# A transformer block's first stage: other engines for its casts and its normalisation, and the next stage's first loads issued inside it

## The chip, the core and the metric

The kernel runs on one core of a Trainium2 chip, as one program. The metric is the device time of one execution in microseconds (us); lower is better. Times here come from several executions of the kernel before and from one more that the hardware profiler recorded.

## What is computed

The input x has 2 sequences of 2048 tokens with 128 features. The first part of the reference is causal attention with 16 heads of 8 features on the layer-normalised x; a mixture-of-experts layer, a scan over time with four-lane attention, and a second mixture-of-experts layer follow, each with a residual connection. The change touches what feeds the attention and the attention's start:

```
xn = layernorm(x)                       # 4096 x 128
q = xn @ Wq.T + bq ;  k = xn @ Wk.T + bk ;  v = xn @ Wv.T + bv
scores = q k^T / sqrt(8), causal
out = softmax(scores) @ v ;  y = out @ Wo.T + bo
```

The product of queries and keys is taken in bf16, with each of q and k split into three bf16 parts (high, middle, low) whose products are summed, so that the result has the precision of float32.

## The kernel before, in words

`hybrid_layer` calls its stages one after the other: `project`, `attend`, `project_out`, then the others. Each stage is a block with one instruction stream for each engine, written by hand; semaphores order them, and an all-engine barrier ends each stage. `stage_semaphores` also clears the semaphores of its stage at its end.

**`project`** works on 8 chunks of 512 tokens (4 tiles of 128). SyncE issues the loads of x (8 chunks, counted on one semaphore for each half), of the weights and of the biases. VectorE takes the statistics of each half (L200, L55 to L61) and the reciprocal of the deviation (L205), whose root is ScalarE's (L251). For each chunk:

- GpSimd normalises x in two instructions (L173 subtracts the mean, L176 multiplies);
- TensorE transposes the four tiles (L290); ScalarE copies the result out of PSUM (L258);
- TensorE projects to q and to k (L295, one matmul of 512 columns each, which runs as two passes) and to v (L299, four matmuls of 128 columns);
- ScalarE writes the high bf16 part of q and of k with bias (L263), and again in float32 (`full`, L265);
- VectorE subtracts the high part from `full` (`rest`, L217), casts it to the middle part (L220), and computes q's low part (L223); GpSimd computes k's (L181);
- VectorE adds the bias to v (L226);
- SyncE stores the three parts of q and of k to DRAM (L133).

TensorE's order for a chunk is: transposes, both projections, values. The loops run dynamically over two times four chunks. The scan's weight is normalised on the side (`norm`, `S_pair`).

**`attend`** goes over 32 heads. For one head, the parts of q and k lie as 48 rows in a stack in SBUF (`Qs`, `Ks`; three stacks in rotation), loaded from DRAM by 12 DMAs (L452). TensorE scores each tile once to find the row maxima (L625, VectorE's L547), and the next time for the exponentials (L615, ScalarE's L593). The maxima pass of head s+1 runs beside the exponentials of head s; for head 0 it runs alone. After 12 of its 40 maxima VectorE reduces and casts them (L523, L526, L528). At the stage's start GpSimd fills buffers (L496, L500), adds the output bias to x in one instruction over 128x4096 elements (L504), and then stages v; TensorE and VectorE wait for all the fills.

The lines that say the order of VectorE's work on a chunk, before:

```
rest[a] = full[a] - parts[a, 0]      # a = 0, 1
parts[a, 1] = rest[a]
parts[0, 2] = rest[0] - parts[0, 1]  # a = 0 only
V = psV + bv_rows
```

## Time and profile before

| | |
|---|---|
| runs | 1838.46, 1840.71, 1843.89 us (median 1840.71) |
| profiled execution, its own time | 1842.67 us |
| its span, first to last instruction | 1840.9 us |
| mean granted TensorE clock | 0.917 of 2.4 GHz |
| busy share: TensorE matmul, VectorE, ScalarE, GpSimd | 84%, 75%, 52%, 34% |
| `project` | 0 to about 69 us |
| `attend` from | 70.31 us |

Times in the profile are microseconds from the span's start. PE is TensorE's matmuls and PEld its weight loads, DVE is VectorE, ACT is ScalarE, POOL is GpSimd, SPq is SyncE's queue. A matmul's end is modelled. PEclk is the granted clock: 1.00 is 2.4 GHz, 0.50 is 1.2 GHz; the record begins at 1.00 and shows no lower value before 56 us, although the first matmuls have the durations of the lower level. Names such as L217 are lines of the kernel.

### The profile page before, as it was taken

The page shows a single profiled execution, that of the slowest core. Times are in us where ns is not written, and L with a number is a line of the kernel's source. Part 1 is how long each engine was busy: PE and PEld are TensorE (multiplying, and loading weights), DVE is VectorE, ACT ScalarE, POOL GpSimd, SP SyncE. Part 2 cuts the span into 40 slices and gives each one's busy share as a digit, 9 for nine tenths or more (in the row PEclk, how much of TensorE's full clock was granted, in tenths as well). Part 3 has the DMA queues.
Part 4 walks back from the last instruction along what each step waited for, and adds up shares of the span by engine and source line. Part 5 has one row for each costly group of instructions (what it writes and reads, how often), then busy time and mean ns, then how long its engine had stood idle before and what let it go on. Part 6 is the DMA issues. An engine that isn't in the chain of part 4 may idle for free. (4 is left out here: it accounts for less than half of the span.)

```text
span 1840.9 us, 42069 instructions
## 1 busy us (share of the span) xinstructions
PE 1552.6 (84%) x13714; PEld 1007.8 (55%) x13714; DVE 1375.7 (75%) x2511; ACT 959.9 (52%) x2309; POOL 630.9 (34%) x430
## 2 busy tenths in 40 slices
PE   4599999999999999999950965999999999975267
PEld 2233333333333333333450955899999999965166
DVE  6799998998998998999261324788888888875222
ACT  4268877887887887888610322344444444431111
POOL 4500000000000000000036332888888888833534
PEclk9689999999999999999955987999999999986588
DMA  3300000000000000000084313011121222104740
GB/s 107 105 19 17 14 20 20 20 20 13 19 20 20 20 20 12 20 20 11 1 272 163 90 35 84 24 46 46 48 54 47 46 46 46 46 12 158 240 123 26
DMA packets 82116, 99.88 MB, mean 54 GB/s; under 512 B 12109, under 2 KB 65482, under 8 KB 81681
## 3 DMA queue, kind: packets, MB, share of 16 engines
q1 hardware_dynamic: 76816, 85.36, 16.0%
q0 software_dynamic: 5120, 12.26, 1.8%
q8 instruction: 97, 1.59, 0.4%
q14 instruction: 83, 0.67, 0.1%
HBM read 43.01 MB, written 31.85 MB: 41 GB/s over the span
## 5 line engine op out<-in xcount | busy, mean ns | idle before, releaser
L547 DVE TENSOR_REDUCE chunk_max<-ps_max 128x1 f32<-128x512 f32 (+3 forms) x1280 | 695.2, 604 | 64.1 <-PE ps_max L642 53.6
L593 ACT ACTIVATE probs<-ps_s 128x512 f32<-128x512 f32 (+3 forms) x1280 | 607.0, 533 | 175.0 <-PE ps_s L634 146.8
L1447 POOL TENSOR_TENSOR lane_products<-L,q 128x1024 f32<-128x1024 f32 x176 | 411.7, 2374 | 119.9 <-POOLq L1254 48.2
L615 PE MATMUL ps_s<-Qs,Ks 50*128 50x512 bf16 (+3 forms) x1280 | 377.2, 354 | 31.7 <-issue 12.1
L625 PE MATMUL ps_max<-Ks,Qs 48*128 48x512 bf16 (+3 forms) x1280 | 386.2, 361 | 12.8 <-POOL Vp L500 10.0
L688 PE MATMUL ps_o<-probs,Vp 128*32 128x512 f32 (+3 forms) x2560 | 344.4, 564 | 3.3 <-ACT probs L593 0.4
L615 PEld LDWEIGHTS ps_s<-Qs,Ks 50*128 50x128 bf16 x1280 | 113.8, 93 | 385.1 <-DVE chunk_max L547 327.6
L511 POOL COPY Vp<-V 128x128 f32 (+1 forms) x32 | 9.6, 300 | 741.2 <-PE ps_o L688 741.2
L1496 DVE TENSOR_TENSOR weighted<-exp_scores,psV_s 128x2048 f32<-128x2048 f32 x88 | 197.0, 2280 | 0.0
L1589 PE MATMUL psZT<-ident,weighted 128*128 128x128 f32 x1408 | 165.7, 273 | 1.8 <-DVE weighted L1496 1.8
L1589 PEld LDWEIGHTS psZT<-ident,weighted 128*128 128x128 f32 x1408 | 156.4, 140 | 2.0 <-DVE weighted L1496 2.0
L1575 PE MATMUL psS<-ident,lane_products 128*128 128x128 f32 x1056 | 128.1, 279 | 3.1 <-POOL lane_products L1447 3.1
L625 PEld LDWEIGHTS ps_max<-Ks,Qs 48*128 48x128 bf16 x1280 | 114.7, 94 | 24.1 <-DVE chunk_max L547 13.0
L1575 PEld LDWEIGHTS psS<-ident,lane_products 128*128 128x128 f32 x1056 | 124.2, 194 | 3.3 <-POOL lane_products L1447 3.3
L642 PE MATMUL ps_max<-ident_b,causal 64*128 64x64 bf16 x1024 | 115.6, 193 | 0.0
L634 PE MATMUL ps_s<-ident_b,causal 64*128 64x64 bf16 x1024 | 114.0, 192 | 0.0
L634 PEld LDWEIGHTS ps_s<-ident_b,causal 64*128 64x128 bf16 x1024 | 93.3, 97 | 23.7 <-issue 2.7
L1633 PE MATMUL psV_s<-S_pair,UT 128*128 128x128 f32 x704 | 97.4, 282 | 1.3 <-DVE weighted L1496 1.0
L642 PEld LDWEIGHTS ps_max<-ident_b,causal 64*128 64x128 bf16 x1024 | 94.5, 99 | 5.5 <-issue 2.0
L1633 PEld LDWEIGHTS psV_s<-S_pair,UT 128*128 128x128 f32 x704 | 85.9, 193 | 9.3 <-ACT UT L1527 7.2
L688 PEld LDWEIGHTS ps_o<-probs,Vp 128*32 128x32 f32 x2560 | 51.1, 109 | 72.2 <-issue 28.3
L1604 PE MATMUL psU<-ident,L 128*128 128x128 f32 x352 | 84.0, 279 | 5.8 <-PEq L1254 3.4
(220 smaller groups left out, 2160.4 us busy)
## 6 DMA issues: line engine op xcount, KB each, us to landing
m_w<-in_L_ffn_w_dram SPq DMA_DIRECT2D x32, 512.0 KB
dispatched<-m_blank SPq DMA_DIRECT2D x2, 4128.0 KB
m_blank<-dispatched SPq DMA_DIRECT2D x16, 516.0 KB
L<-q SPq DMA_DIRECT2D x16, 448.0 KB
Qs<-q_parts SPq DMA_DIRECT2D x192, 32.0 KB
Ks<-k_parts SPq DMA_DIRECT2D x192, 32.0 KB
L<-q SPq DMA_DIRECT2D x20, 192.0 KB
L<-q SPq DMA_DIRECT2D x28, 128.0 KB
```

Of the source, the lines that this page charges most:

```text
L547: nc.vector.tensor_reduce(out, scores[:, 0:w], axis=AX.X, op=ALU.max).then_inc(max_reduced, 1)
L593: nc.scalar.activation(dst, ps_s[(k + r) % R][:, q0:], ACT.Exp, scale=SCALE).then_inc(exp_done, 1)
L615: last = nc.tensor.matmul(ps_s[(k + r) % R][:, q0:], K[r][rows, kt * P:(kt + 1) * P], Q[r][rows, g * QW + q0:(g + 1) * QW], start=True, st ...
L625: last = nc.tensor.matmul(ps_max[(k + r) % R][:, 0:w], Q[r][rows, i * P:(i + 1) * P], K[r][rows, ck * QW:ck * QW + w], start=True, stop=no ...
L634: last = nc.tensor.matmul(ps_s[(k + r) % R][:, q0:q0 + HALF], c.causal[rows, 0, half, :], c.ident_b[rows, rows], start=False, stop=half == 1)
L642: last = nc.tensor.matmul(ps_max[(k + r) % R][:, k0:k0 + HALF], c.causal[rows, 1, half, :], c.ident_b[rows, rows], start=False, stop=half ...
L688: last = nc.tensor.matmul(ps_o[32 * q:32 * q + 32, q0:], Vp[r][:, kt, cols], src, start=first and not odd, stop=last_batch and odd)
L1447: return nc.gpsimd.tensor_tensor(out[:, l].rearrange("p (j m) d -> p j m d", m=LA), c.L[ch][:, :, l * LW:(l + 1) * LW].unsqueeze(2).broadc ...
L1496: nc.vector.tensor_tensor(weighted[v][:, rows], expd[:, :, rows].rearrange("p l r -> p r l").unsqueeze(3) .broadcast_to([P, ROWS // 2, LA, ...
L1575: nc.tensor.matmul(psS[:, 0:P], products[:, :, d], c.ident[:], start=d == PART, stop=False, is_transpose=True)
L1589: last = nc.tensor.matmul(psZT[:, j * P:(j + 1) * P], weighted[u][:, j * LA + m, :, :].rearrange("p l d -> p (l d)"), c.ident[:], start=m ...
L1633: last = nc.tensor.matmul(psV[:, j * D:(j + 1) * D], c.UT[u][:, j * P:(j + 1) * P], c.S[:, 0, :], start=True, stop=True)
```

## The change

In `project`:

- x is normalised by VectorE, one instruction for each tile of 128 tokens (`normalise`, in the new kernel L218), instead of by GpSimd. Chunks 0 and 1 are normalised ahead of the loop, chunk n+2 behind the values of chunk n.
- ScalarE no longer writes `full`; VectorE takes the rest directly from PSUM (scalar_tensor_tensor: PSUM plus bias, minus high part, L226). ScalarE casts the rest to the middle part.
- GpSimd computes the low part of both q and k.
- TensorE transposes chunk n+1 ahead of projecting chunk n.
- Loads of x are counted chunk by chunk; the second half's come behind the weights; the rows of the value bias come last. The second half's statistics stand behind the normalisation of the first two chunks. The table of ScalarE's functions is loaded once.
- The loops are unrolled, and buffers are waited for only once they have been used.
- SyncE issues the loads of heads 0, 1 and 2 at the stage's end, behind its stores.

In `attend` those loads go, the buffers' fills are in another order, VectorE waits for the first three of them only, and TensorE for none until head 0's exponentials. The stacks and their semaphores are now taken with the attention's tensors (`attention_tensors`), whose own scope ends after `project_out`.

```diff
+def load_head(sp, c, q_parts, k_parts, s, r, p):
+    rows, cols = bass.ds(s % H * HD, HD), bass.ds(s // H * T, T)
+    for stack, parts, order in ((c.Q[r], q_parts, (0, 0, 0, 1, 1, 2)), (c.K[r], k_parts, (0, 1, 2, 0, 1, 0))):
+        for row, a in enumerate(order):
+            sp.dma_start(stack[p * HALF + row * HD:p * HALF + (row + 1) * HD, :], parts[a, rows, cols])\
+              .then_inc(c.stacks_loaded[r], 16)
...
         @block.sync
...
+            load_x(0)
             for m, w in enumerate((Wq, Wk, Wv, Wo)):
                 sp.dma_start(W_nat[:, m, :], w).then_inc(w_loaded, 16)
...
+            load_x(1)
             sp.dma_start(bv_rows[:], bv.rearrange("(a d) -> a d", a=1).broadcast_to([P, D])).then_inc(b_loaded, 16)
...
+            for k in range(SLOTS):
+                sp.wait_ge(stored[k], 32)
+            for s in range(STACKS):
+                load_head(sp, c, q_parts, k_parts, s, s, s % 2)
+            for k in range(SLOTS):
+                sp.wait_ge(stored[k], 32 * (NCH // SLOTS))
...
         @block.gpsimd
...
             for ch in range(NCH):
-                if ch + 2 < NCH:
-                    normalise(ch + 2, ch % 2)
-                last_part(ch, ch % 4)
+                for a in range(2):
+                    part = parts[ch % SLOTS]
+                    pool.wait_ge(mid_done, 2 * ch + a + 1)
+                    nc.gpsimd.tensor_tensor(part[:, a, 2, :], rest[ch % 2][:, a, :], part[:, a, 1, :], ALU.subtract)\
+                      .then_inc(lo_done, 1)
...
         @block.vector
...
+            def normalise(ch):
+                dve.wait_ge(rstd_done, ch // CB + 1)
+                if ch >= 2:
+                    dve.wait_ge(xT_in_psum, ch - 1)
+                for i in range(TC):
+                    t = ch * TC + i
+                    last = nc.vector.tensor_scalar(xn[ch % 2][:, i, :], c.X[:, t, :], mean[:, t:t + 1],
+                                                   rstd[:, t:t + 1], ALU.subtract, ALU.mult)
+                last.then_inc(xn_ready, 1)
...
+                nc.vector.scalar_tensor_tensor(out=rest[ch % 2][:, a, :], in0=psQK[ch % 2][a][:],
+                                               scalar=bias_cols[:, a:a + 1], in1=parts[ch % SLOTS][:, a, 0, :],
+                                               op0=ALU.add, op1=ALU.subtract).then_inc(rest_done, 1)
...
+            for ch in range(NCH):
+                for a in range(2):
+                    rest_of(ch, a)
+                values(ch)
...
+                if ch + 2 < NCH:
+                    normalise(ch + 2)
...
         @block.scalar
...
+            act.wait_ge(b_loaded, 64)
+            copy_tokens(0)
+            for ch in range(NCH):
...
+                for a in range(2):
+                    act.wait_ge(qk_in_psum, 2 * ch + a + 1)
+                    nc.scalar.activation(part[:, a, 0, :], psQK[ch % 2][a][:], ACT.Identity,
+                                         bias=bias_cols[:, a:a + 1]).then_inc(hi_done, 1)
+                if ch + 1 < NCH:
+                    copy_tokens(ch + 1)
+                for a in range(2):
+                    act.wait_ge(rest_done, 2 * ch + a + 1)
+                    nc.scalar.activation(part[:, a, 1, :], rest[ch % 2][:, a, :], ACT.Copy).then_inc(mid_done, 1)
...
         @block.tensor
...
+            for ch in range(NCH):
+                if ch + 1 < NCH:
+                    turn(ch + 1)
+                pe.wait_ge(xT_copied, ch + 1)
...
 # attend
-            for t, value in [(t, 0.0) for t in Vp] + [(t, LEAST) for t in chunk_max] + [(probs0, 0.0), (ones_row, 1.0)]:
+            for t, value in [(t, LEAST) for t in chunk_max] + [(ones_row, 1.0)] + [(t, 0.0) for t in Vp] + [(probs0, 0.0)]:
...
-            dve.wait_ge(made, MADE)
+            dve.wait_ge(made, R)
...
-            pe.wait_ge(made, MADE)
```

Three places of the instruction order. First VectorE, one chunk in the steady state; what stands in brackets are the semaphores that the instruction waits for. Before:

```order
L217 TENSOR_TENSOR rest<-full,parts 128x512 [waits project_full_done]
L220 CAST parts<-rest 128x512 [waits project_rest_done]
L222 REGISTER_ALU
L223 TENSOR_TENSOR parts<-rest,parts 128x512 [waits project_mid_done]
L216 REGISTER_ALU
L217 TENSOR_TENSOR rest<-full,parts 128x512 [waits project_full_done]
L220 CAST parts<-rest 128x512 [waits project_rest_done]
L225 REGISTER_ALU
L226 ISA [waits project_v_in_psum]
L226 TENSOR_TENSOR V<-psV,bv_rows 128x4x16x8
```

The same for the new kernel, a chunk and the start of the next:

```order
L226 SCALAR_TENSOR_TENSOR rest<-psQK,bias_cols,parts 128x512 [waits project_lo_done,project_hi_done] x2
L232 TENSOR_TENSOR V<-psV,bv_rows 128x4x16x8 [waits project_v_in_psum]
L218 TENSOR_SCALAR xn<-X,mean,rstd 128x128 [waits project_xT_in_psum,project_rstd_done]
L218 TENSOR_SCALAR xn<-X,mean,rstd 128x128 x3
L226 SCALAR_TENSOR_TENSOR rest<-psQK,bias_cols,parts 128x512 [waits project_lo_done,project_hi_done] x2
```

Casts and q's low part have left VectorE; four normalisations, of the chunk two ahead, stand behind the addition for the values.

Second TensorE, over one chunk in the steady state of the new kernel (chunk 2's work with chunk 3's transposes, and the transposes of chunk 4):

```order
L317 MATMUL psT<-ident,xn 128x128 [waits project_xT_copied,project_xn_ready]
L317 MATMUL psT<-ident,xn 128x128 x3
L330 MATMUL psQK<-xnT,W_T 128x512 [waits project_rest_done,project_xT_copied]
L330 MATMUL psQK<-xnT,W_T 128x512
L337 MATMUL psV<-W_T,xnT 128x128 [waits project_v_done]
L337 MATMUL psV<-W_T,xnT 128x128 x3
L317 MATMUL psT<-ident,xn 128x128 [waits project_xT_copied,project_xn_ready]
```

The kinds and their sequence are those of before, but the transposes are now those of the chunk ahead of the one projected behind them.

Third SyncE, at the end of the new stage and the start of `attend`:

```order
L148 DMA k_parts<-parts 128x3x512 [waits project_lo_done]
L75 DMA Qs<-q_parts 8x2048 [waits project_stored2,project_stored3,project_stored1,project_stored0]
L75 DMA Qs<-q_parts 8x2048 x5
L75 DMA Ks<-k_parts 8x2048 x6
L75 DMA Qs<-q_parts 8x2048 x6
L75 DMA Ks<-k_parts 8x2048 x6
L75 DMA Qs<-q_parts 8x2048 x6
L75 DMA Ks<-k_parts 8x2048 x6
L88 UNCONDITIONAL_BRANCH [waits project_stored2,project_stored3,project_stored1,project_stored0]
L483 UNCONDITIONAL_BRANCH [waits barrier_Pool_Activation_PE_DVE_SP_release]
L509 DMA Ks<-ones_row 2x2048 [waits project_b_loaded]
```

The 36 loads of three heads stand between the last store and the barrier; before, 24 stood behind the barrier and 12 further down.

## Rows read from the trace of the kernel before

**Rows 1.** A stretch: its length; PE, PEld, DVE, ACT, POOL busy us (count); clock; DMA share, GB/s

```profile
40.00:50.00 10.00, 7.05 (x32) 4.29 (x32) 9.83 (x11) 6.20 (x12) 7.39 (x6) 1.00 0.45 158
```

**Rows 2.** Time line, stage end: start, us, engine, line, operation [idle before]; then a wait

```profile
64.46 1.16 POOL L181 TENSOR_TENSOR parts<-rest,parts 128x512 bf16<-128x512 f32 x1 [2.88 <-DVE parts L220]
66.11 0.49 SPq L133 DMA_DIRECT2D k_parts<-parts  x1
70.31 2.06 SPq L452 DMA_DIRECT2D Qs<-q_parts  x6
...
SPq L136 <- DMA k_parts<-parts: 2.5, 1, 2.5
```

**Rows 3.** Time line of the start, and one stretch

```profile
7.50 1.96 DVE L200 BATCH_NORM_STATS2 st<-X  x8 [7.50 <-DMA X<-in_L_attn_a_x_dram]
11.65 0.19 DVE L55 TENSOR_TENSOR tmp<-st 128x16 f32<-128x16 f32 x1
14.03 0.25 DVE L205 RECIPROCAL rstd<-std 128x16 f32<-128x16 f32 x1 [1.29 <-ACT std L251]
22.32 3.77 PE L295 MATMUL psQK<-xnT,W_T 128*128 128x512 f32 x4 [4.63 <-ACT xnT L258]
...
13.00:14.00 1.00, 0.35 (x3) 0.26 (x2) 0.00 (x0) 0.91 (x3) 0.00 (x0) 1.00 0.35 21
```

**Rows 4.** Time line, one chunk at the higher clock, and projections four chunks later

```profile
30.98 0.60 PE L290 MATMUL psT<-ident,xn 128*128 128x128 f32 x4
32.48 1.98 PE L295 MATMUL psQK<-xnT,W_T 128*128 128x512 f32 x4 [0.89 <-ACT xnT L258]
33.63 0.69 ACT L263 ACTIVATE parts<-psQK,bias_cols 128x512 bf16<-128x512 f32 x1 [1.29 <-PE psQK L295]
...
50.71 1.98 PE L295 MATMUL psQK<-xnT,W_T 128*128 128x512 f32 x4 [0.76 <-ACT xnT L258]
```

**Rows 5.** Time line, VectorE and GpSimd in one chunk

```profile
39.82 0.68 DVE L226 TENSOR_TENSOR V<-psV,bv_rows 128x512 f32 x1
39.98 1.16 POOL L181 TENSOR_TENSOR parts<-rest,parts 128x512 bf16<-128x512 f32 x1 [1.69 <-PE psT L290]
40.42 1.27 DVE L217 TENSOR_TENSOR rest<-full,parts 128x512 f32<-128x512 f32 x1
41.10 1.49 POOL L173 TENSOR_TENSOR centred<-X,mean 128x512 f32<-128x512 f32 x1
```

**Rows 6.** Time lines and a group, a later stage's normalisation beside GpSimd and alone

```profile
933.95 1.82 DVE L968 TENSOR_SCALAR m_rows<-X,m_mean,m_rstd 128x128 f32<-128x128 f32 x1 [1.75 <-POOL m_up_to L928]
935.63 1.89 POOL L932 COPY m_rows<-X 128x2048 f32<-128x2048 f32 x1
935.69 2.43 DVE L968 TENSOR_SCALAR m_rows<-X,m_mean,m_rstd 128x128 f32<-128x128 f32 x3
1116.72 3.58 DVE L1315 TENSOR_SCALAR U<-X,mean_b,rstd_b 128x128 f32<-128x128 f32 x13
```

**Rows 7.** Groups: xcount | busy us, mean ns | idle before

```profile
L1045 DVE SCALAR_TENSOR_TENSOR m_y<-m_psY,m_blank 128x128 f32<-128x128 f32 x64 | 19.5, 347 | 79.6 <-PE m_psY L1180 63.6 <-issue 16.0
L1067 ACT ACTIVATE m_work<-m_expd 128x256 f32<-128x256 f32 x4 | 1.7, 414 | 0.0
```

**Rows 8.** Stretches of TensorE alone: busy us (count), clock, DMA share, GB/s

```profile
56.75:57.50 0.75, 0.75 (x2) 0.50 0.00 0
60.50:61.25 0.75, 0.23 (x3) 1.00 0.19 64
63.50:64.25 0.75, 0.00 (x0) 0.52 1.09 384
```

**Rows 9.** Time line of the attention's start

```profile
76.20 0.61 PE L625 MATMUL ps_max<-Ks,Qs 48*128 48x512 bf16 x1 [9.97 <-POOL Vp L500]
76.22 8.82 POOL L504 TENSOR_TENSOR X<-X,bo_rows 128x4096 f32<-128x4096 f32 x1
83.21 1.86 DVE L526 CAST neg_max_b<-neg_max 128x8 bf16<-128x8 f32 x1
```

More of the change, by code:

```diff
@@ L86, in project @@
         mean, var, std, rstd = (sb(n, [P, NT]) for n in ("mean", "var", "std", "rstd"))
[L87 removed]
         xn = [sb(f"xn{u}", [P, TC, D]) for u in range(2)]
         xnT = [sb(f"xnT{u}", [P, CH]) for u in range(2)]
[L90 removed]
         rest = [sb(f"rest{u}", [P, 2, CH]) for u in range(2)]
[L92 removed]
+        parts = [sb(f"parts{k}", [P, 2, 3, CH], bf16) for k in range(SLOTS)]
         squares = sb("squares", [P, D])
@@ L202, in _, with statistics @@
+            def statistics(b):
+                for ch in range(b * CB, (b + 1) * CB):
+                    dve.wait_ge(x_loaded[ch], 16)
+                    for i in range(ch * TC, (ch + 1) * TC):
+                        nc.vector.bn_stats(st[:, i:i + 1, :], c.X[:, i:i + 1, :]).then_inc(stats, 1)
                 dve.wait_ge(stats, (b + 1) * NB)
-                finish_stats(nc, steps, st[:, half, :], tmp[:, :, half], mean[:, half], var[:, half])
+                finish_stats(nc, steps, st[:, half[b], :], tmp[:, :, half[b]], mean[:, half[b]], var[:, half[b]])
@@ new lines, in invert @@
+                nc.vector.reciprocal(rstd[:, half[b]], std[:, half[b]]).then_inc(rstd_done, 1)
+            def normalise(ch):
[7 more added lines that the diff above has]
+                last.then_inc(xn_ready, 1)
@@ L231, in _ @@
+            statistics(0)
+            invert(0)
+            dve.wait_ge(wT_in_psum, 1)
+            nc.vector.tensor_copy(W_T[:].rearrange("p m d -> p (m d)"), psT[0][:, 0:3 * D]).then_inc(wT_copied, 1)
+            nc.vector.tensor_copy(c.Wo_T[:], psT[0][:, 3 * D:]).then_inc(wT_copied, 1)
+            normalise(0)
+            normalise(1)
             dve.wait_ge(norm_act, 2)
@@ L302, in _, with turn @@
-            pe.wait_ge(norm_dve, 2)
-            pe.wait_ge(xT_copied, NCH + 2)
-            nc.tensor.transpose(psT[0][:, 0:D], c.S[:, 0, :], c.ident[:]).then_inc(norm_pe, 1)
+            def turn(ch):
+                pe.wait_ge(xn_ready, ch + 1)
+                if ch >= 2:
+                    pe.wait_ge(xT_copied, ch - 1)
+                for i in range(TC):
+                    last = nc.tensor.transpose(psT[ch % 2][:, i * P:(i + 1) * P], xn[ch % 2][:, i, :], c.ident[:])
+                last.then_inc(xT_in_psum, 1)
@@ new lines, in _ @@
+            pe.wait_ge(wT_copied, 2)
+            turn(0)
+            pe.wait_ge(norm_act, 2)
+            for ch in range(NCH):
+                if ch + 1 < NCH:
+                    turn(ch + 1)
+                pe.wait_ge(xT_copied, ch + 1)
+                if ch >= 2:
+                    pe.wait_ge(rest_done, 2 * (ch - 2) + 2)
+                for a in range(2):
+                    nc.tensor.matmul(psQK[ch % 2][a][:], W_T[:, a, :], xnT[ch % 2][:], start=True, stop=True)\
+                      .then_inc(qk_in_psum, 1)
+                if ch >= 2:
+                    pe.wait_ge(v_done, ch - 1)
+                if ch == 1:
+                    pe.wait_ge(norm_dve, 3)
+                for i in range(TC):
+                    last = nc.tensor.matmul(psV[ch % 2][:, i * D:(i + 1) * D], xnT[ch % 2][:, i * P:(i + 1) * P],
+                                            W_T[:, 2, :], start=True, stop=True)
+                last.then_inc(v_in_psum, 1)
+                if ch == 0:
+                    pe.wait_ge(norm_dve, 2)
+                    nc.tensor.transpose(psV[1][:, 0:D], c.S[:, 0, :], c.ident[:]).then_inc(norm_pe, 1)
@@ L446, in _ @@
         def _(sp):
-            def load(s, j, r, p):
-                rows, cols = bass.ds(s % H * HD, HD), bass.ds(s // H * T, T)
-                for stack, parts, order in ((Q[r], q_parts, (0, 0, 0, 1, 1, 2)), (K[r], k_parts, (0, 1, 2, 0, 1, 0))):
-                    for row, a in enumerate(order):
-                        sp.dma_start(stack[p * HALF + row * HD:p * HALF + (row + 1) * HD, :], parts[a, rows, cols])\
-                          .then_inc(stacks_loaded[r], 16)
             def place_max_rows(s, j, r, p, f):
@@ L483, in _ @@
             place_max_rows(0, 0, 0, 0, 1)
-            load(2, 0, 2, 0)
             place_max_rows(1, 0, 1, 1, 0)
```

189 lines of the change are left out of this document (64 added, 125 removed).

## The prediction

> **What bounds the kernel now.** I looked first at stretches of ten microseconds, to place the change. The first stage fills 70 of 1840.9 us. From 40 to 50 us TensorE is busy 7.05 us of 10; VectorE shows 9.83 and GpSimd 7.39 [rows 1], but part of that is waiting inside instructions, as the time line will show. So what counts is who waits for whom.
>
> Then SyncE's queue, for the end of the stage. The last GpSimd subtraction ends at 65.6 (64.46 + 1.16); the last store is issued by 66.6, SyncE waits 2.5 us for its landing, and the attention's first instructions start at 70.31: from the last subtraction to the next stage 4.7 us. The head loads behind it are issued six in 2.06 us, 0.34 each, four such groups [rows 2].
>
> Then the time line from the start. VectorE begins its statistics at 7.50, when four chunks of x have landed together; the reciprocal is at 14.03; the first projection starts at 22.32, because ScalarE's copy waits for the second half's statistics. Loads still move between 13 and 14 us, at a share of 0.35 [rows 3].
>
> Last, one chunk at the higher clock (2.4 GHz): transposes at 30.98, projections at 32.48, first cast 1.15 us after their start. Four passes in 1.98 us less a tail of 0.26 are 0.43 each, so the second tensor's result can be cast at 1.15 + 0.86 = 2.0. Four chunks later the projections start at 50.71: 4.6 us a chunk [rows 4].
>
> **The part that decides: VectorE and GpSimd exclude each other.** At 40.42 VectorE's subtraction of two SBUF operands lasts 1.27 us (the values' addition of the same size has 0.68), because GpSimd's subtraction runs until 41.14. GpSimd's next, already due, (41.10) then lasts until 42.59, 0.9 after VectorE's end: it ran only once VectorE was through. They take turns. The addition from PSUM at 39.82 keeps its 0.68 beside GpSimd [rows 5]. The case nearest to the new code is later in the program: two GpSimd copies of 1.88 us back to back against the same kind of normalisation (TENSOR_SCALAR, 128x128, two scalars from columns). The first normalisation waits out the first copy, the second normalisation waits out the second copy (the copy, starting 935.63, follows after one normalisation only), then they run at 0.27 us [rows 6]. So a GpSimd instruction that is due gets in between two of VectorE's.
>
> **The change, part by part.**
> Start. Chunks are counted one by one, so at 7.50 only the last four tiles are left: 1.0 us (eight take 1.96), then seven small instructions of 0.19, with their waits 1.1, and 0.5 for root and reciprocal: 10.1. The weights' two copies, also 512 columns from PSUM, 0.8 with 0.68 for the values as measure; four normalisations 1.1: first transposes at 12.0. ScalarE waits for the bias rows, now the last loads; the bytes are the same, so about 14.2. Copy 0.6: first projections 14.9, 7.4 us earlier than 22.32. The one table load less lies before the loads land: nothing. The first projections last 3.77 us, twice the 1.98 of later ones [rows 3, 4]: the durations of the lower level, 1.2 GHz, whatever the clock column says there. So the second cast comes at +3.8, rest 1 ends at 20.1, the values are issued by 20.7, and the third chunk is normalised behind two GpSimd subtractions: its transposes start at 23.4.
>
> The cycle. TensorE now transposes chunk n+2 ahead of projecting n+1; the transposes need the normalisation, which VectorE issues behind the values of chunk n, which need chunk n's last matmuls. So the next chunk cannot start while this one runs, although its operands for the projection are ready. From the transposes' start, higher clock [rows 4]: projections 0.5; second cast 2.5 to 3.2; rest 1 to 3.9; values issued until 4.5. The new rest has one operand from PSUM and one from SBUF, as the values: 0.68 at least; at most 0.86, which is 0.35 for the 128-column form plus three quarters of 0.68; I take 0.68. Meanwhile ScalarE copies tokens (3.1 to 3.7) and casts the middle parts from SBUF: no row has that form; 256 columns from SBUF take 0.41, so 0.41 to 0.83, taken 0.65, near the 0.69 of the cast from PSUM [rows 4, 7]. They are ready at 4.2 and 4.8. GpSimd's two third parts (1.16 each) then occupy 4.3 to 6.6. One normalisation slips in between, the other three end 0.65 after them, and the transposes start at **7.3 us**. With VectorE unhindered it would be 5.6 (4.5 + 1.1).
>
> The trace has 0.27 us from one normalisation to the next, 0.34 for one alone [rows 6]. The Trainium skill (VectorE: DVE Perf Modes, section on the TRN2 errata) gives 58 + elements/2 cycles for the doubled mode, 0.13 us here; by an estimate from it the three left would end 0.3 earlier, and the forecast would be 1861. The trace disagrees, and I use its 0.27.
>
> The clock. In such a cycle TensorE works 3.2 us and idles 4.1. It fell from 1.00 at 63.5 us after idling from 60.8, and at 56.7 within the old cycles [rows 8]. The first projections took 3.8 us at the lower level before the work behind them was fast [rows 3]. A cycle that falls costs 0.4 more for the transposes and, with the clock back after 3.8 us of work, 1.5 more for the projections: 9.2 us; wholly at the lower level 9.5. I take a fall in about three of four cycles: 8.7. Five cycles from 23.4: 66.9. After the last transposes nothing is normalised any more: chunk 7's copy ends at +3.7, its projections start at 3.8, its second cast at 5.8, its first middle part is ready at 7.1, and GpSimd's last two subtractions end at 9.3 (11.2 with a start at the lower clock, 13.4 wholly at it). Third parts end at **78.1**.
>
> The head loads. They sit on SyncE behind the last stores and before its end of the stage, so the barrier waits for their issue: 36 x 0.34 = 12.2 us. The landing of the last store (2.5) is hidden under them. From the last third part: 0.1 + 0.5 + 12.2 + 1.2 = 14.0 us, against 4.7 before. The attention starts at **92.1** instead of 70.31: +21.8.
>
> The attention. TensorE starts at once, not 5.9 us after the barrier (76.20 behind the memsets). But VectorE's small cast after the first 12 maxima comes 7.0 us after TensorE's start, and GpSimd's addition of bo (8.82 us) starts 5.9 us after the barrier as before. Before, both began together and the cast ended with it, at 85.07, 14.8 after the barrier [rows 9]; now the cast arrives at 7.0, finds the addition running for 1.1 us, and again ends at 14.8. What follows is VectorE's row of maxima, unchanged. So the early start is worth nothing. The load of head 2 that leaves SyncE's later queue waited for nobody: nothing. The semaphores taken with the attention's tensors add a clearing and a barrier behind the output projection: no row alone; between nothing (in the shadow of the one there) and 1.2 (the whole passage at 70.31), taken 0.5.
>
> **Sum:** start -7.4, first projections to the last third part 63.2 instead of 43.3, +19.9, passage +9.3, barrier +0.5: **+22.3 us**. The profiled execution took 1842.67 (span 1840.9), 2 above the runs' median 1840.71; on the median this is **1863.0**. Some 0.3% (5.5 us) is what a measurement of this kernel can tell from no change.
>
> **Rivals.**
> (a) The same, but the clock stays up: 7.3 us a cycle, third parts end at 69.2, +13.4, 1854. For it: in the old cycles of 4.6 us it held 1.00 from 40 to 50 us [rows 1]. Against: it fell in the end [rows 8], and the spans are now of 4.1. Chance 0.17.
> (b) VectorE's four normalisations go as one block once it has its turn: only one subtraction is waited out, and the cycle is 6.45 at the higher clock (5.45 + 0.1 + 0.8 + 0.1), 0.85 less, six times: +17, 1858. Against it the alternation in [rows 6]. 0.10.
> (c) No mutual wait in this pair at all (the form from columns does not hold what GpSimd needs): 5.5 us a cycle, full clock, third parts at 58.9, +3, 1844. Against: [rows 6]. 0.10.
> (d) The other side, faster: as (c) with cycles of 5.3 (rest 1 being the only limit; -1.2), and the attention's first cast gets through before GpSimd's addition, because VectorE no longer waits for the memsets. It decides if the cast arrives under 5.9 us after the barrier, where I count 7.0; then head 0's maxima end 7.7 earlier: 1835. 0.08.
> (e) The whole stage at the lower clock: 9.5 a cycle, third parts at 84.3, +28.5, 1869; it belongs to the forecast's spread.
>
> **Numbers.** Forecast with (e) 0.55. 1863 is its likeliest time. Range 1847 to 1871: it takes in (a), (b) and (e), leaves out (c) and (d), 0.18, and has room for the bounds of the small costs: rest up to 0.18 more on six cycles, 1.1; the casts, whose subtractions end later or earlier by 0.2, 1.4 either way; the barrier -0.5 to +0.7. Faster by over 0.3% is (d), 0.08; within 0.3% (c), 0.10; slower the rest, 0.82.
>
> **What would show it.** First projections at about 15 us. Then projections every 7 to 9.5 us, with VectorE's normalisations of 1 us and more where 0.34 is their length, GpSimd's subtractions in pairs before each, and TensorE idle by about 4 us on the normalisation. A granted clock of 0.50 in much of 20 to 80 us. 36 head loads in one row of 12 us with all engines still behind them, and a cast of some 8 us at the attention's start. Wrong would be: projections closer than 6 us, normalisations all of 0.34, head loads issued before the last chunk's stores, or a first cast of 0.2 us.

## The result, and the profile after

| | before | after |
|---|---|---|
| runs, median (lowest to highest) | 1841.91 us (1838.46 to 1843.89) | 1868.50 us (1865.84 to 1871.44) |
| span of the profiled execution | 1840.9 us | 1868.5 us |
| mean granted TensorE clock | 0.917 | 0.907 |

Ratio 1.0143, 95% interval 1.0126 to 1.016: slower, and inside the predicted range. The forecast of 1863.0 is 5.5 us low. The parts below show that this is a smaller error than it deserves: the steps it described came out 4 to 5 us smaller together, and one of 10 us was not in it at all.

**The start.** Time line of the changed kernel, the first statistics to the first projections (start, us, engine, line, operation, idle before):

```profile
3.54 2.64 DVE L204 BATCH_NORM_STATS2 st<-X 128x6 f32<-128x128 f32 x12 [3.54 <-DMA X<-in_L_attn_a_x_dram]
6.49 0.87 DVE L204 BATCH_NORM_STATS2 st<-X 128x6 f32<-128x128 f32 x4 [0.31 <-DMA X<-in_L_attn_a_x_dram]
8.83 0.25 DVE L210 RECIPROCAL rstd<-std 128x16 f32<-128x16 f32 x1 [0.35 <-ACT std L271]
10.86 2.11 PE L317 MATMUL psT<-ident,xn 128*128 128x128 f32 x8 [1.20 <-DVE xn L218]
12.39 0.60 ACT L277 ACTIVATE xnT<-psT 128x512 f32<-128x512 f32 x1 [2.52 <-DMA bo_rows<-in_L_attn_a_bo_dram]
...
13.04 3.78 PE L330 MATMUL psQK<-xnT,W_T 128*128 128x512 f32 x4
```

Chunks counted one by one put the reciprocal at 8.83 instead of 14.03 [rows 3]. ScalarE's copy then waits for the bias rows, as foreseen, but they land at 12.4 and not at 14.2. First projections at 13.04: 9.3 us earlier than before.

**A cycle.** Time line of the changed kernel, chunk 3 at a granted clock of 1.00:

```profile
39.52 0.66 PE L317 MATMUL psT<-ident,xn 128*128 128x128 f32 x4 [3.83 <-DVE xn L218]
40.02 1.88 PE L330 MATMUL psQK<-xnT,W_T 128*128 128x512 f32 x4
...
41.80 1.61 DVE L226 SCALAR_TENSOR_TENSOR rest<-psQK,bias_cols,parts 128x512 f32<-128x512 f32 x2 [2.34 <-ACT parts L292]
...
43.33 0.68 DVE L232 TENSOR_TENSOR V<-psV,bv_rows 128x512 f32<-128x512 f32 x1
43.71 2.26 POOL L192 TENSOR_TENSOR parts<-rest,parts 128x512 bf16<-128x512 f32 x2 [4.84 <-ACT parts L298]
43.93 2.64 DVE L218 TENSOR_SCALAR xn<-X,mean,rstd 128x128 f32<-128x128 f32 x4
...
46.62 0.66 PE L317 MATMUL psT<-ident,xn 128*128 128x128 f32 x4 [3.83 <-DVE xn L218]
```

From transposes to transposes 7.10 us (46.62 - 39.52). TensorE is idle for 3.83 of them, on a normalisation. Four normalisations that would last 1.1 us take 2.64: they end 0.6 us after GpSimd's pair (43.71 + 2.26), so three of the four come behind it. The stretches of three cycles (length; PE, PEld, DVE, ACT, POOL busy; clock; DMA share, GB/s):

```profile
30.80:39.50 8.70, 4.89 (x16) 2.97 (x16) 4.66 (x7) 2.90 (x5) 2.26 (x2) 0.81 0.25 89
39.50:46.60 7.10, 3.27 (x16) 2.12 (x16) 4.66 (x7) 2.90 (x5) 2.26 (x2) 1.00 0.31 111
46.60:54.80 8.20, 4.96 (x17) 3.09 (x17) 4.63 (x7) 2.90 (x5) 2.26 (x2) 0.78 0.28 98
```

VectorE, ScalarE and GpSimd do the same work in each; what differs is TensorE's busy time and its granted clock. The six transposes behind the first two chunks start at 21.55, 30.80, 39.52, 46.62, 54.78 and 63.47: cycles of 9.25, 8.72, 7.10, 8.16 and 8.69, mean 8.38.

**The passage and the attention's start.** Time lines of the changed kernel, GpSimd, SyncE's queue, TensorE and VectorE (these answer to [rows 2] and [rows 9]):

```profile
71.56 2.26 POOL L192 TENSOR_TENSOR parts<-rest,parts 128x512 bf16<-128x512 f32 x2 [0.80 <-ACT parts L298]
...
73.85 0.37 SPq L148 DMA_DIRECT2D k_parts<-parts  x1
74.40 2.13 SPq L75 DMA_DIRECT2D Qs<-q_parts  x6
...
84.68 1.99 SPq L75 DMA_DIRECT2D Ks<-k_parts  x6
...
88.23 0.33 POOL L523 MEMSET chunk_max<- 128x64 f32 x3 [14.41 <-POOLq L88]
88.45 0.58 PE L650 MATMUL ps_max<-Ks,Qs 48*128 48x512 bf16 x1 [17.45 <-DVEq L545]
94.15 8.80 POOL L531 TENSOR_TENSOR X<-X,bo_rows 128x4096 f32<-128x4096 f32 x1
95.44 7.54 DVE L553 CAST neg_max_b<-neg_max 128x8 bf16<-128x8 f32 x1
```

Six groups of six head loads occupy SyncE's queue from 74.40 to 86.7, with nothing running on the other engines; the attention starts at 88.2, 14.4 us behind the last third part (73.8) and 17.9 later than before. The cast ends at 102.98, 14.8 behind the barrier, to the tenth the distance of before.

**Not in the forecast: the attention itself takes 10 us longer.** GpSimd copies one head's columns of V per head, and these copies are a clock for the 32 heads. Time line of GpSimd around a jump back to the start of the loop over six heads, the kernel before and then the changed one:

```profile
253.62 0.30 POOL L511 COPY Vp<-V 128x128 f32 x1 [24.18 <-PE ps_o L688]
283.15 0.30 POOL L511 COPY Vp<-V 128x128 f32 x1 [29.23 <-PE ps_o L688]
307.63 0.30 POOL L511 COPY Vp<-V 128x128 f32 x1 [24.17 <-PE ps_o L688]
```

```profile
271.80 0.30 POOL L538 COPY Vp<-V 128x128 f32 x1 [24.19 <-PE ps_o L714]
304.15 0.30 POOL L538 COPY Vp<-V 128x128 f32 x1 [32.06 <-PE ps_o L714]
328.65 0.30 POOL L538 COPY Vp<-V 128x128 f32 x1 [24.20 <-PE ps_o L714]
```

A head takes 24.48 us in both kernels. The head with the jump takes 29.53 before (5.05 more) and 32.35 after (7.87 more). The four jumps cost 5.05 + 4.53 + 5.20 + 3.98 = 18.8 us before and 7.87 + 7.06 + 6.93 + 7.07 = 28.9 after. TensorE's own time line at the last jump of the changed kernel:

```profile
757.18 0.38 PE L640 MATMUL ps_s<-Qs,Ks 50*128 50x512 bf16 x1 [3.23 <-issue]
...
757.63 0.19 PE L659 MATMUL ps_s<-ident_b,causal 64*128 64x64 bf16 x1
760.12 0.21 PE L667 MATMUL ps_max<-ident_b,causal 64*128 64x64 bf16 x1 [2.30 <-issue]
```

There are two stalls in which TensorE waits for no other engine ("issue"), nine matmuls apart. The kernel before has one at each of its four jumps, of 2.96 to 3.09 us; the changed kernel has a second one behind each, of 1.75 to 2.30 us.

The profile's view of the DMA queues shows what is waited for. It has a queue for instructions (q8), in packets of 16 KB each, about one for every 110 of TensorE's matmuls. Its line for the whole kernel before, then for the whole changed kernel, then for the changed kernel from 757.20 to 760.10 us, the second stall (queue, kind: packets, MB, share):

```profile
q8 instruction: 97, 1.59, 0.4%
q8 instruction: 101, 1.65, 0.4%
q8 instruction: 1, 0.02, 2.3%
```

Around the last jump of the changed kernel a packet starts at 754.1, before TensorE goes on at 757.18; the next one starts at 757.8, and TensorE stands until 760.12. In the kernel before, the packets at the last jump start at 728.9 and 732.0, TensorE goes on at 731.79, and nothing waits for the second. So the code behind a jump back is loaded again, and the block behind it is asked for only once TensorE is running; a loop that starts shortly before a block's end then waits a second time.

So the sum of the traces is +17.9 at the attention's start, +10.1 at the jumps, +0.5 at the barrier behind the output projection (from VectorE's last addition to the next stage 1.35 us instead of 0.90) and -0.9 elsewhere: +27.6, the difference of the spans.

### The profile page after: what moved, and what is told of

It is laid out like the page before. It is cut to its first block and busy times, and to the rows that moved or that the text cites. A ratio compares the mean times of both kernels' runs of the same rounds, so it can differ in the third digit from the quotient of the medians.

```text
span 1868.5 us, 41903 instructions
## 1 busy us (share of the span) xinstructions
PE 1562.6 (84%) x13714; PEld 1013.3 (54%) x13714; DVE 1376.0 (74%) x2519; ACT 957.1 (51%) x2308; POOL 620.8 (33%) x422
## 5 line engine op out<-in xcount | busy, mean ns | idle before, releaser
L650 PE MATMUL ps_max<-Ks,Qs 48*128 48x512 bf16 (+3 forms) x1280 | 386.4, 361 | 25.9 <-DVEq L545 17.4
L714 PEld LDWEIGHTS ps_o<-probs,Vp 128*32 128x32 f32 x2560 | 51.3, 109 | 72.4 <-issue 28.6
```

Of the source, the lines that this page charges most:

```text
L650: last = nc.tensor.matmul(ps_max[(k + r) % R][:, 0:w], Q[r][rows, i * P:(i + 1) * P], K[r][rows, ck * QW:ck * QW + w], start=True, stop=no ...
L714: last = nc.tensor.matmul(ps_o[32 * q:32 * q + 32, q0:], Vp[r][:, kt, cols], src, start=first and not odd, stop=last_batch and odd)
```

## The experiments

"Changed kernel" is the one predicted. The comparisons ran on chips whose median for the kernel before was between 1841.9 and 1846.3, so I compare ratios to it; with its 1.0143 the changed kernel would have had 1871.4 beside the first four runs, 1872.7 beside the next four and 1870.9 beside runs 9 to 11.

The sum of the four jumps, in every trace, by where the loop over heads starts in TensorE's program (my count of instructions):

| kernel | loop starts at | four jumps, us | packets of instructions (q8) |
|---|---|---|---|
| before | 825 | 18.8 | 97 |
| changed | 940 | 28.9 | 101 |
| e1_pad84 | 1024 | 19.6 | 98 |
| e2_pad141 | 1081 | 19.7 | 98 |
| e3_before_pad115 | 940 | 28.8 | 101 |
| e4 to e8 | 940 | 27.6 to 28.4 | 101 in each |
| e9, e10 | 1024 | 19.0, 18.3 | 98, 98 |
| e11, e12 | 980 | 17.4, 19.4 | 97, 98 |

Each sum is from one trace. The kernels with the start at 940 begin their attention anywhere from 63.8 us (run 5) to 89.1 us (run 4) and cost the same at the jumps, so the time at which the attention starts doesn't matter.

**1. 84 more instructions for TensorE.**

```diff
+            for _ in range(168):
+                pe.wait_ge(made, 1)
             pe.wait_ge(made, 7)
             pe.wait_ge(w_loaded, 80)
```

> The changed kernel with 84 more TensorE instructions (168 waits on a count long reached, paired by the compiler) at the very start of TensorE's program; nothing else moves. By my count the loop over six heads then starts 1024 instructions into TensorE's program instead of 940. Theory, position of code: the 10.4 us that the attention lost came at the four jumps back to the loop's start, because TensorE's instructions are fetched in blocks and the loop now starts at another place of one. Then the stalls at the jumps change again: the shift of the max-row loads from the first loop pass to the last, 10.1 us in the changed kernel, becomes another number (0 to 8), and the time falls by up to 10 us (about 1859 to 1866 us; the padding itself may cost 0 to 3 us in the first stage). Rival, timing or layout of data (the other start of the attention, other tensor addresses, DMA contention): all of that is unchanged here, so the stalls stay two of 2.3 to 3.4 us per jump and the time stays 1868 to 1871.

Measured 1863.76 us, ratio 1.0098 (1.008 to 1.0116), 7.6 less than the changed kernel and inside the expected 1859 to 1866. The jumps cost 9.3 less. The waits themselves are not free: the weights' transposes start at 10.24 instead of 7.65 and the attention 2.0 later.

**2. 141 more (282 waits).**

> The same with 141 more instructions: the loop starts at 1081, which has the remainder of the kernel before (57) if blocks hold 256. Theory, position of code with blocks of 256: one stall of about 3.2 us per jump as before the change, the attention's own length back within 1 us of that before (the shift of the max-row loads constant at about 18), time 1858 to 1862. Rival, position matters but not with that period: some other number of stalls. Rival, timing or data layout: 1868 to 1872 and two stalls per jump.

Measured 1874.45 us, ratio 1.0162 (1.0142 to 1.0182). The time was missed, because I took the padding for nearly free: the weights' transposes start at 16.39, 8.7 us late. In the attention the theory holds: one stall for each jump, 9.2 us less.

**3. The kernel before with 115 more (230 waits).**

> The kernel before with 115 more TensorE instructions at the start of TensorE's program: its loop over heads then starts at 940 instructions, exactly where the changed kernel's does by my count. Theory, position of code: two stalls per jump as in the changed kernel, and the time rises by about 10 us, to 1850 to 1853. Rival, timing or data layout: 1841 to 1843, since nothing but those waits is different, and they end before the weights have landed.

Measured 1853.40 us, ratio 1.0043 (1.0026 to 1.006): 8.4 us more by the medians, 11.3 by the spans of the traces. This one decides: nothing of the change is in it, and its four jumps cost 28.8 us, 10.0 more than in the kernel before. The expectation that the added waits end before the weights have landed was wrong: the weights' transposes start at 14.50 instead of 12.04, and the attention 2.3 us later, which is most of the rest of the 11.3. Time line of TensorE at its last jump, with both stalls of the changed kernel, the second ten matmuls behind the first:

```profile
741.40 0.39 PE L617 MATMUL ps_s<-Qs,Ks 50*128 50x512 bf16 x1 [3.54 <-issue]
...
744.35 0.23 PE L636 MATMUL ps_s<-ident_b,causal 64*128 64x64 bf16 x1 [2.22 <-issue]
```

So the 10 us come from where the code lies; the other start of the attention, other tensor addresses and the head loads, which this kernel has as before, aren't needed for them.

**4. The addition of bo behind all heads.**

```diff
-            nc.gpsimd.tensor_tensor(c.X[:], c.X[:], c.bo_rows[:].unsqueeze(1).broadcast_to([P, NT, D]), ALU.add)
...
             sections(pool, section)
+            nc.gpsimd.tensor_tensor(c.X[:], c.X[:], c.bo_rows[:].unsqueeze(1).broadcast_to([P, NT, D]), ALU.add)
```

> The changed kernel, with GpSimd's addition of bo to X (8.8 us) moved behind all its sections of the attention. Theory, VectorE and GpSimd take turns: VectorE's cast behind the first twelve maxima lasts 0.2 us instead of 7.54 and ends 7.4 us after the barrier instead of 14.8; head 0's maxima, and all behind them, come 7 to 7.5 us earlier; time 1861. Rival, what follows is limited by something else (the head loads, TensorE): the cast is short, but the time changes by less than 2 us. Second rival, the addition collides with VectorE's work elsewhere: up to 9 us come back at the place where it now stands, time 1861 to 1870.

Measured 1871.06 us, ratio 1.0144 (1.0123 to 1.0165): nothing won. The expectation was missed. The first cast lasts 0.17 us and the max-row loads come 6.5 to 7.7 us earlier than in the changed kernel, but near the end this is given back, as the second rival said. Time line, GpSimd and VectorE at the last heads:

```profile
856.34 8.85 POOL L540 TENSOR_TENSOR X<-X,bo_rows 128x4096 f32<-128x4096 f32 x1
...
858.90 6.31 DVE L552 CAST neg_max_b<-neg_max 128x8 bf16<-128x8 f32 x1
```

In both places tried, an instruction of 8.8 us covers one of VectorE's small casts.

**5. The normalisation ahead of the rests.**

```diff
             for ch in range(NCH):
+                if ch + 2 < NCH:
+                    normalise(ch + 2)
                 for a in range(2):
                     rest_of(ch, a)
                 values(ch)
...
-                if ch + 2 < NCH:
-                    normalise(ch + 2)
```

> The changed kernel, with VectorE's normalisation of chunk n+2 moved ahead of chunk n's rests (it stood behind chunk n's values). My account of the cycle (the next transposes wait for a normalisation that stands behind the values, which stand behind this chunk's last matmuls): the chain is cut, the next transposes are ready while this chunk projects, and the cycle falls from 8.4 us in the mean to 4.3 to 5.0; the third parts end 20 to 24 us earlier, at 50 to 54 us, and the time is 1845 to 1849. Rival, the turns between VectorE and GpSimd are the real limit and not the order: the normalisations still last 2.4 us a group and now delay the rests by as much, the cycle is 6.5 to 7.5, and 6 to 12 us are won (1857 to 1862). Rival, the clock: TensorE stays at the lower level for most of the stage and a cycle takes 5 to 6 us.

Measured 1844.08 us, ratio 0.9987 (0.9978 to 0.9997), 28.6 less than the changed kernel. Time line of TensorE and VectorE, and the whole stretch of the cycles:

```profile
31.56 0.66 PE L317 MATMUL psT<-ident,xn 128*128 128x128 f32 x4 [1.00 <-DVE xn L218]
...
33.34 2.43 DVE L218 TENSOR_SCALAR xn<-X,mean,rstd 128x128 f32<-128x128 f32 x4
...
35.82 0.66 PE L317 MATMUL psT<-ident,xn 128*128 128x128 f32 x4 [1.00 <-DVE xn L218]
```

```profile
18.70:44.00 25.30, 19.87 (x97) 12.90 (x98) 24.59 (x43) 17.91 (x32) 13.62 (x12) 1.00 0.46 163
```

The cycle is 4.26 us (35.82 - 31.56), and the last third part ends at 49.4 instead of 73.8. A group of normalisations still takes 2.43 us: VectorE and GpSimd still wait for each other, but that wait no longer stands on TensorE's chain. TensorE idles 1.0 us in a cycle and its granted clock stays at 1.00, which is the 2.4 GHz level. That order alone costs 24.4 us (the attention starts at 63.8 and not 88.2), more than the change loses up to that point.

**6. No third parts.**

```diff
-            for ch in range(NCH):
-                for a in range(2):
-                    part = parts[ch % SLOTS]
-                    pool.wait_ge(mid_done, 2 * ch + a + 1)
-                    nc.gpsimd.tensor_tensor(part[:, a, 2, :], rest[ch % 2][:, a, :], part[:, a, 1, :], ALU.subtract)\
-                      .then_inc(lo_done, 1)
+            for part in parts:
+                nc.gpsimd.memset(part[:, :, 2, :], 0.0).then_inc(lo_done, 1)
```

> The changed kernel without GpSimd's sixteen subtractions of the third parts (the third parts are zero, written once; all stores and products stay, so the low parts of q and k are left out of the scores). Theory, the two engines take turns: with no GpSimd instruction in the way the four normalisations last 1.1 us a group instead of 2.3 to 2.6; the cycle is 7.3 - 1.7 = 5.6 us at the higher clock and 7 to 7.5 with a fall; mean about 6.5 against 8.4. Six cycles give 9 to 13 us, the last third part 2.3 us more: time 1853 to 1858. Rival, the normalisations are slow by themselves (a form that lasts 0.6 us each): groups stay at 2.3 us and more, only the tail of 2.3 us is won, 1865.

Measured 1861.15 us, ratio 1.0073 (1.0056 to 1.009), 11.6 less than the changed kernel. Time line of its cycle at the higher clock:

```profile
29.33 0.66 PE L314 MATMUL psT<-ident,xn 128*128 128x128 f32 x4 [2.37 <-DVE xn L215]
...
33.73 1.11 DVE L215 TENSOR_SCALAR xn<-X,mean,rstd 128x128 f32<-128x128 f32 x4
34.90 0.66 PE L314 MATMUL psT<-ident,xn 128*128 128x128 f32 x4 [2.30 <-DVE xn L215]
```

SyncE's stores and VectorE's rests then wait for the middle parts, since the low parts come from no instruction of the loop. The four normalisations take 1.11 us: the form is fast by itself, and the 1.5 us of each group were GpSimd's. The cycle is 5.57 (34.90 - 29.33); expected was 5.6. The mean of five is 6.87, because the clock fell in the others as it did in the changed kernel.

**7. The head loads back in the attention.**

```diff
-            for s in range(STACKS):
-                load_head(sp, c, q_parts, k_parts, s, s, s % 2)
...
+            load_head(sp, c, q_parts, k_parts, 0, 0, 0)
+            load_head(sp, c, q_parts, k_parts, 1, 1, 1)
```

Head 2's stands behind head 0's max rows, as in the kernel before.

> The changed kernel with its 36 head loads issued in the attention stage, as the kernel before has them; all else stays. Theory, the loads only hold the barrier: the passage from the last third part to the attention's start falls from 14.4 us to about 4.9 and nothing is lost behind it, since the first cast waits for GpSimd's addition in either case: 9.5 us earlier, 1859. Rival, what the early loads gain is real and hidden elsewhere: TensorE's first maxima come 5.9 us after the barrier again, and the time changes by less than 4 us.

Measured 1862.10 us, ratio 1.0072 (1.0051 to 1.0094), 10.6 less than the changed kernel. From the last third part to the attention 4.0 us in place of 14.4. Its first stage was slower in the trace (a clock of 0.67 from 20 to 70 us where the changed kernel's trace has 0.80; the last transposes 3.8 us later), so only 6.0 us of the 10.4 show at the attention's start there; with one trace of each kernel it is open whether the execution or the edit made that difference. Its five cycles take 8.8 to 9.3 us, all with a fall of the clock. TensorE's first maxima come 6.0 us behind the barrier here, and the cast waits for the addition again and ends 14.8 us behind it, as with the early loads.

**8. The addition of bo beside the head loads.** It stands behind GpSimd's last third part, with waits for the bias rows and for the last normalisation.

> The changed kernel, with GpSimd's addition of bo (8.8 us) put behind its last third part, in the first stage, while SyncE issues the 36 head loads (12.3 us) and all other engines are idle. Theory: there it costs nothing, the first cast of the attention lasts 0.2 us instead of 7.54, all behind it comes 7.4 us earlier and, other than when the addition stood at the attention's end, nothing is lost later: 1861. Rival, the addition collides with the loads for SBUF or delays the barrier: less than 4 us won.

Measured 1864.12 us, ratio 1.0093 (1.0076 to 1.0109), 8.6 less. The addition runs from 73.83 to 82.63, while SyncE issues loads until 86.7; the attention starts at 88.4; the first cast lasts 0.17 us.

**9 and 10. All of it together.** Run 9 has the edit of run 5; head 0's loads behind chunk 4's stores and head 1's behind chunk 5's; bo in six pieces; 21 tiny products behind TensorE's last values. Run 10 is the same with the loads of run 7.

```diff
+                if ch in (4, 5):
+                    for k in range(SLOTS):
+                        sp.wait_ge(stored[k], 32)
+                    load_head(sp, c, q_parts, k_parts, ch - 4, ch - 4, ch - 4)
...
+                    if not isinstance(s, int) and (r, p) == (0, 1):
+                        add_bo((j - 1) * 3, 6)
+                else:
+                    add_bo(30, 2)
...
+            pe.wait_ge(rest_done, 2 * NCH - 2)
+            for _ in range(21):
+                nc.tensor.matmul(psQK[0][0][:, 0:1], ones[:], norm[:, 0:1], start=True, stop=True)
```

> The changed kernel with what the runs so far point to: the normalisation ahead of the rests; bo added in pieces (five of 768 columns, 1.7 us each, right behind a copy of V's columns where VectorE reads PSUM only, and one of 256); the loads of heads 0 and 1 issued behind the stores of chunks 4 and 5, those of head 2 in the attention; and 21 tiny products (84 instructions) at the end of TensorE's first stage, so that the loop over heads starts at instruction 1024. If the four causes add: attention starts at about 54 us (63.8 less 9.5), the first cast is 0.2 us (7.4 less), the loop's jumps cost 19 us in sum instead of 29: against the kernel before 6.6 + 9.5 + 7.4 less, +0 for the jumps, 1820 to 1824, ratio 0.987. Rivals: the addition's pieces or the early loads collide with VectorE or the stores (1827 to 1835); the fast start frees nothing because the attention's first stores or loads are late (over 1835).

> The same, with all head loads in the attention stage as the kernel before has them. It shows what head loads in the first stage are worth where they don't hold the barrier. Theory, nothing much: TensorE's first maxima come about 2 to 6 us later behind the barrier, since twelve loads are issued (4.1 us) and land first, and nothing else covers it now that the addition of bo is gone: 2 to 6 us longer than with them early. Rival: 0, because VectorE waits for GpSimd's fills anyway.

Measured 1820.41 us, ratio 0.9882 (0.9854 to 0.9909), and 1824.01 us, ratio 0.9898 (0.9872 to 0.9925): the four causes add. The pieces of 1.82 us cost nothing that shows: the copy of V right behind each comes after 24.48 or 24.49 us like the others. (Three later heads of run 9 took 0.3 us more; run 10, with the same pieces, has none over 0.13.) Head loads in the first stage are worth 3.6 us by the medians where they don't hold the barrier (2.3 by the first maxima, which start at 56.88 against 59.13); the intervals of the two ratios overlap, so that gain is small and only likely.

**11. 40 more instructions in the changed kernel.**

> The changed kernel with 40 more TensorE instructions at the start, so that its loop over heads starts at 980. By the theory of blocks of 256 instructions the loop's start then lies 44 instructions before a block's end; with 84 left (the changed kernel) the jumps cost 28.9 us in sum, with 199 or 256 left 19 to 20. Theory: the second block is needed even sooner than with 84 left, so the second stall is at least as long: 29 to 33 us in sum. Rival, the number of instructions left is not what decides: 19 to 20 us.

Measured 1859.94 us, ratio 1.0091 (1.0063 to 1.0119), 11.0 less than the changed kernel, and 17.4 us for the four jumps: the expectation was wrong. What decides isn't the distance to a block's end as I counted it, that is with a block of 256 instructions ending at 1024. Two things fit each other: in the changed kernel and in run 3 the second stall comes nine or ten matmuls (some 20 instructions with their weight loads) behind the jump's target, so a block would end near 960 by my count; a loop that starts at 980 lies just past it. My count would then be off by about 64 from the chip's. The packets of instructions say the same. Behind the jump there are three: for the target, for the next block, and a third once TensorE is in that next block. The third starts 27 matmuls behind the jump in all seven kernels with the start at 940, after 82 to 85 with a start at 825 or 1081, after 84 to 111 at 1024 and after 113 to 131 at 980. With ends at 960 and every 256 from there, the starts lie 20, 135, 192 and 236 instructions ahead of one: the same order. No run tested a start between 940 and 980.

**12. Head 0's loads alone, loop start at 980.** Run 9 with `if ch == 4`, head 1's loads in the attention, and 10 products.

> The combined kernel again, with only head 0's twelve loads in the first stage (behind chunk 4's stores) and head 1's at the start of the attention, and with 10 tiny products instead of 21 at the end of TensorE's first stage, so that the loop over heads starts at instruction 980. In the combined kernel the last stores were issued 2.4 us late, behind head 1's loads; here they go out at once: the attention starts 2 to 2.4 us earlier, and head 1's loads land long before they are needed. The jumps: with the start at 980 they cost 17.4 us in sum in one run, with 1024 19.0 to 19.6. If the position decides, it is 17 to 18 here too, and the time 1816 to 1818 (ratio 0.985 to 0.987). Rival, the 17.4 were chance: 19 to 20 in sum and 1818 to 1820; rival, the loads of head 1 now hold TensorE: as long as the combined kernel or longer.

Measured 1816.79 us, ratio 0.9862 (0.9846 to 0.9879). The best version: 1.4% faster than the kernel before and 2.8% faster than the changed one (0.9862 / 1.0143 = 0.972). Time line of GpSimd and VectorE at its attention's start:

```profile
46.85 2.27 POOL L192 TENSOR_TENSOR parts<-rest,parts 128x512 bf16<-128x512 f32 x2 [0.62 <-ACT parts L298]
53.13 0.33 POOL L528 MEMSET chunk_max<- 128x64 f32 x3 [4.01 <-POOLq L88]
...
60.30 0.17 DVE L564 CAST neg_max_b<-neg_max 128x8 bf16<-128x8 f32 x1
```

The attention starts 17.2 us earlier than in the kernel before (53.13 against 70.31). The jumps cost 19.4 us: the start at 980 doesn't give 17.4 by itself, as the rival said. What made run 11's sum smaller is open.

## Why the prediction was right, and where it was not

| term | predicted | measured |
|---|---|---|
| first projections | 14.9 (-7.4) | 13.04 (-9.3) |
| cycle at the higher clock | 7.3 | 7.10 |
| cycle, mean | 8.7 | 8.38 |
| rest; middle cast | 0.68; 0.65 | 0.75; 0.63 |
| last third part ends | 78.1 | 73.8 |
| passage | 14.0 | 14.4 |
| attention starts | 92.1 (+21.8) | 88.2 (+17.9) |
| first cast ends, behind the barrier | 14.8 | 14.8 |
| attention | +0 | +10.1 |
| barrier behind the output projection | +0.5 | +0.5 |
| elsewhere | 0 | -0.9 |
| sum, profiled execution | +22.3 | +27.6 |

**Right: the chain.** The transposes wait for a normalisation queued behind the values; run 5 takes that order away and nothing else, and the cycle falls to 4.26.

**Right: the mutual wait.** Rival (c) had none; run 6, without GpSimd's instructions, has normalisations of 1.11 us a group where the changed kernel has 2.6. The detail holds too: one of four slips in between GpSimd's pair and three follow it. Rival (b), the group as one block, would have had 6.45 us for the 7.10.

**Right, a little high: the clock.** The cycles with a fall took 8.2 to 9.25 us where 9.2 to 9.5 was said, and four of five had one; the granted clock from 20 to 70 us was 0.80 in the mean. Rival (e), the lower level throughout, didn't happen either: the third parts ended at 73.8 and not at its 84.3. That 1868.50 lies on its 1869 is chance. Rival (a), the clock stays up, didn't happen in the changed kernel. It happened in run 5, with a cycle in which TensorE idles 1.0 us instead of 3.8.

**Right: the head loads.** They hold the barrier by their issue, 0.34 us each; run 7 takes 10.4 us from the passage. **Right: the first cast.** The early start of TensorE was worth nothing because GpSimd's addition ended at the same distance: 14.8 us behind the barrier with it and, in run 7, without it; run 8 moves the addition and wins 8.6.

**Mis-sized: the start.** The step "about 14.2" took the bias rows to land as late as all loads did in the kernel before; they landed at 12.4. (The reciprocal came at 8.83 and not by 10.1, because the statistics began at 3.54 and not at 7.50, but the bias rows hid that.) With the shorter cycles and a tail of 10.35 us (63.47 to 73.82) where 11.2 stood in the sum, the last third part came 4.3 us earlier than said.

**Wrong: no term for the loop over heads.** Behind the first cast the prediction takes the attention as "unchanged", without a reason for TensorE's jumps. That held for what the instructions do and for whom they wait for; not for how they are fetched. The change replaced TensorE's rolled loop over chunks by straight code (115 instructions more by my count ahead of the loop over heads), and that moved this loop to a place where each jump back stalls twice. Run 3 gives the kernel before the same 10 us with waits alone. The profile of before did show one stall for each jump ("issue", 3.1 us at most), and nothing in the prediction asks what it depends on. Without this the changed kernel would have taken about 1858 us, and the forecast of 1863 would have been 4.8 us too high by the spans: two errors of opposite sign stand in the sum. Both times lie in the stated range, so that the measured one lies there says little of the parts.

## What to carry to other kernels

Write down for each engine what its next instruction waits for, and ask of every instruction queued ahead of it whether it must be there: here a call that was due stood behind one that wasn't, and moving it won 24 us of the first stage, more than the whole change lost there. Loads issued early are early only if nothing waits for their issue, and a long GpSimd instruction that excludes VectorE belongs where VectorE has nothing to do, or in pieces between VectorE's small instructions. After a change that grows or shrinks an engine's code, compare the time of one pass of every later loop, and of its jumps, also where the loop itself was not touched.

## What the runs showed of the hardware that was not expected

- The cost of a jump back depends on where the loop lies in TensorE's program: 17.4 to 19.7 us for four jumps in seven kernels (starts at 825, 980, 1024 and 1081), 27.6 to 28.9 in seven kernels with the start at 940. The second stall is there at each of the 28 jumps of the latter, 1.3 to 2.7 us long, and at none of the others, and the granted clock is lower behind it: 0.77 from 755 to 770 us, around the changed kernel's last jump, against 0.89 from 730 to 745 in the kernel before. In all a jump costs 2.5 us more (10.1 over four).
- The Trainium skill (Runtime: NRT & Kernel Launch, section on instruction fetch mechanics) says that instructions come in blocks of 16 KiB, 256 instructions, prefetched in order, and that a taken branch to a target outside the pages at hand waits for a fetch. The traces agree: packets of 16 KB, one that starts some 3 us before TensorE goes on behind each jump, and a third packet that comes at the same distance for starts 256 apart (825 and 1081). What these runs add is that the block behind the target is asked for only 0.2 to 0.8 us after TensorE goes on, so that a block's end some 20 instructions behind the target costs a second stall. By the packets an end lies near 960 by my count; no run places it more closely.
- 168 satisfied waits, 84 instructions by my count, started the weights' transposes 2.6 us later; 282, or 141 instructions, 8.7 us. Satisfied waits are code too.
